# Layer 0's rotation of K: one product less, and its swapped half made by four SyncE copies; K cut a step sooner, Q a step later

## The reference

```python
Q = (query @ Wq.T).reshape(B, Tq, N_HEADS, D_K).transpose(0, 2, 1, 3)
K = (key @ Wk.T).reshape(B, Tk, N_HEADS, D_K).transpose(0, 2, 1, 3)
V = (value @ Wv.T)...
def apply_rope(x, cos, sin):
    x1 = x[..., 0::2]
    x2 = x[..., 1::2]
    r1 = x1 * c - x2 * s
    r2 = x1 * s + x2 * c
Q = apply_rope(Q, cos_q, sin_q)
K = apply_rope(K, cos_k, sin_k)
scores = jnp.einsum('bhqd,bhkd->bhqk', Q, K) / math.sqrt(D_K)
attn = jax.nn.softmax(scores, axis=-1)
out = jnp.einsum('bhqk,bhkd->bhqd', attn, V)
return out.transpose(0, 2, 1, 3).reshape(B, Tq, D_MODEL) @ Wo.T
```

## Time and profile before

| | |
|---|---|
| time, median of 3 runs | 532.25 us (531.01 to 532.5) |
| time of the profiled execution | 530.89 us |
| its span, first to last instruction | 529.1 us |
| mean granted TensorE clock | 0.947 |
| busy: PE, PE weight loads | 453.4 us (86%), 348.9 us (66%) |
| busy: DVE, ACT, POOL | 377.4 (71%), 348.2 (66%), 336.8 us (64%) |
| SyncE's DMA queue | 95666 packets, 45.06 MB, 34.6% of 16 engines |

### The profile page before, as it was taken

How to read it: one execution, slowest core, us unless ns; L and a number is a source line. 1 busy time by engine, 2 the same in 40 slices (tenths; PEclk the granted TensorE clock), 3 DMA queues, 4 the chain that set the end, 5 groups by cost and what they waited for, 6 DMA issues and landing times.

```text
span 529.1 us, 19004 instructions
## 1 busy us (share of the span) xinstructions
PE 453.4 (86%) x6103; PEld 348.9 (66%) x6103; DVE 377.4 (71%) x1113; ACT 348.2 (66%) x892; POOL 336.8 (64%) x710
## 2 busy tenths in 40 slices
PE   2688899999987888998799999999988615999992
PEld 2456677777765777997456666566655405999991
DVE  6787887888888557864567888898987562555551
ACT  4356788888876455664267788788875714666660
POOL 5787987788763346766444674888887670555552
PEclk9788999999999999999789999999998956999996
DMA  7556455555551720453222232243331133444430
GB/s 180 144 138 157 116 143 129 139 130 144 132 123 43 242 45 1 78 118 92 59 53 61 75 75 70 78 109 100 95 83 60 64 121 92 108 107 107 106 99 21
DMA packets 99108, 53.43 MB, mean 101 GB/s; under 512 B 25235, under 2 KB 96035, under 8 KB 99027
## 3 DMA queue, kind: packets, MB, share of 16 engines
q1 hardware_dynamic: 95666, 45.06, 34.6%
q0 software_dynamic: 2784, 6.82, 3.7%
q10 hardware_dynamic: 576, 0.53, 0.4%
HBM read 17.89 MB, written 8.81 MB: 50 GB/s over the span
## 4 chain that ended last, share of the span: by engine, by line
PE 62%; DVE 10%; DMA 9%; issue 6%; POOL 6%; SPq 3%; ACT 2%; ACTq 0%; DVEq 0%; POOLq 0%
PE bank L738 10%; PE bank L965 6%; PE score L686 6%; PE scoreT L955 4%; DMA stack<-negpT 4%; PE bank L873 4%; DVE negmax L1603 4%; PE scoreT L863 3%; DMA stack<-pieces 3%; PE score L651 3%; PE bank L787 3%; PE bank L600 3%; PE score L955 2%; PE scoreT L661 2%; PE scoreT L713 2%
## 5 line engine op out<-in xcount | busy, mean ns | idle before, releaser
L1603 DVE TENSOR_REDUCE negmax<-score 128x8 f32<-128x1024 f32 x128 | 156.3, 1221 | 46.2 <-PE score L686 45.2
L1077 ACT ACTIVATE P<-scoreT 128x1024 f32<-128x1024 f32 x128 | 131.2, 1025 | 48.2 <-PE scoreT L704 26.6
L738 PE MATMUL bank<-P,Vc 128*32 128x128 f32 x2048 | 71.7, 282 | 1.3 <-issue 0.8
L1517 POOL DMA_INDIRECT out<-by x39 | 37.4, 960 | 48.2 <-DVE by L1963 47.2
L738 PEld LDWEIGHTS bank<-P,Vc 128*32 128x32 f32 x2048 | 53.8, 112 | 15.5 <-issue 12.1
L686 PE MATMUL score<-stack 64*128 64x128 bf16 x896 | 45.8, 223 | 8.6 <-DMA stack<-pieces 4.3
L686 PEld LDWEIGHTS score<-stack 64*128 64x128 bf16 x896 | 26.1, 96 | 38.7 <-issue 22.1
L1358 POOL TENSOR_TENSOR negp<-negmax,blank 128x16 bf16<-128x16 f32 x64 | 14.1, 220 | 55.5 <-DVE negmax L1603 53.9
L965 PE MATMUL bank<-M,P 128*128 x312 | 41.4, 276 | 0.5 <-DVE by L1963 0.5
L1250 ACT ACTIVATE P<-scoreT,We 128x128 f32<-128x128 f32 x104 | 29.7, 369 | 15.3 <-PE scoreT L955 15.3
L965 PEld LDWEIGHTS bank<-M,P 128*128 128x128 f32 x312 | 38.0, 192 | 0.7 <-issue 0.7
(11 more groups left out here) (220 smaller groups left out, 1210.2 us busy)
## 6 DMA issues: line engine op xcount, KB each, us to landing
stack<-pieces SPq DMA_DIRECT2D x96, 128.0 KB, 2.6
stack<-pieces SPq DMA_DIRECT2D x96, 64.0 KB
XB<-expert_rows SPq DMA_DIRECT2D x39, 66.0 KB, 1.9
XA<-expert_rows SPq DMA_DIRECT2D x39, 64.0 KB, 1.9
XR<-in_x SPq DMA_DIRECT2D x4, 512.0 KB, 4.7
ctxT<-in_ctxT SPq DMA_DIRECT2D x16, 128.0 KB, 2.3
stack<-blank SPq DMA_DIRECT2D x32, 64.0 KB, 2.2
stack<-negpT SPq DMA_DIRECT2D x64, 32.0 KB, 1.9
```

Of the source, the lines that this page charges most:

```text
L738: mm = nc.tensor.matmul(PVOUT[VCOL * i:VCOL * (i + 1), half * 128:(half + 1) * 128], Vc[:, k % BODY, at:at + VCOL], P32[:, 2 * p_slot(L, k ...
L1077: nc.scalar.activation(P32[:, at:at + 2, :], SCORET[:], ACT.Exp, scale=SCALE).then_inc(sem("exp_done"), 1)
L1517: nc.gpsimd.indirect_dma_start(out=out, out_offset=bass.IndirectOffsetOnAxis(ap=at_, axis=0), in_=by[r][:, 0:D], in_offset=None).then_inc( ...
L1603: nc.vector.tensor_reduce(negmax[:, k % 2, :, half * HQ:(half + 1) * HQ], SCORE[:].rearrange("p r (h k) -> p r h k", h=HQ), AX.X, ALU.max, ...
```

## The change

K's product with the swapped weights is gone. The channels of a head are laid out even ones first (`EVEN_FIRST`), so that a channel's neighbour lies 32 partitions away. VectorE multiplies K's one product by a table with the opposite sign (`sinN`, a new input and load) and by cosT, the sine first. SyncE then copies the four blocks of 32 partitions of the sine product into a new tile `turned`, each block into its neighbour's place (`turn_keys`), and GpSimd adds `rotA` and `turned`. Q keeps two products.

K's product is written two steps sooner in the program and its cut one; Q's cut is one step later; the stack slots that need only K's later pieces go first. The context load is two steps sooner and waits for the value product of batch t + 4. The transposes of the normalised x move from the middle of the odd step to the end of the even one; ScalarE's work on them and on V moves accordingly. VectorE's cut of the first K is gone. SyncE's loop runs one round less, with the rest written out.

```diff
@@ SyncE
                         if L == 0:
-                            sp.wait_ge(sem("k_pieces"), middle)
+                            sp.wait_ge(sem("k_pieces"), low)
+                        sp.wait_ge(sem("q_pieces"), middle)
                         for s in LAST_SLOTS:
...
+                def turn_keys(k):
+
+                    p = pair(k)
+                    if is_pair(p):
+                        sp.wait_ge(sem("k_rotated"), known(2 * p + 1))
+                        sp.wait_ge(sem("k_full"), known(p + 0))
+                        for to in range(0, 128, TURN):
+                            at = to ^ TURN
+                            sp.dma_start(turned[to:to + TURN, :], rot[at:at + TURN, 3, :]).then_inc(sem("k_turned"), 16)
...
                     max_rows(t + 1, j + 1)
+                    if L == 0 and isinstance(t, int) and t == -AHEAD:
+                        load_ctx(j + 8)
                     if j % 2 == 1:
                         if L == 0:
-                            load_ctx(j + 7)
+                            turn_keys(j + 7)
+                            load_ctx(j + 9)
                             load_adj(j - 1)
@@ TensorE
-                def project_k(k, half):
+                def project_k(k):
...
+                        pe.wait_ge(sem(f"ctx_loaded{L}{b}"), 16 * turns(k))
+                        pe.wait_ge(sem("q_rotated"), 2 * p)
+                        nc.tensor.matmul(QK[:, 0:PAIR], W0[:, 2, :], ctxT[b][:], start=True, stop=True).then_inc(sem("k_projected"), 1)
...
-                    if L == 0 and j % 2 == 1:
-                        xn_transposes(j + 7, t)
...
-                        project_k(j + 6, 0)
-                        project_k(j + 6, 1)
+                        project_k(j + 8)
+                        xn_transposes(j + 8, t)
@@ ScalarE
-                        high(j + 4, 1)
+                        high(j + 4, 0)
+                        normalise(j + 8, (0, 1) if isinstance(t, int) and t == -AHEAD else (1,))
                     elif L == 0:
-                        high(j + 5, 0)
+                        high(j + 5, 1)
+                        evac_xnT(j + 7, t)
@@ GpSimd
                         pool.wait_ge(sem(f"{nm}_rotated"), 2 * p + 2)
+                        if which == 1:
+                            pool.wait_ge(sem("k_turned"), 64 * p + 64)
...
-                        cut(j + 4, 1)
+                        cut(j + 4, 0)
                     else:
-                        cut(j + 5, 0)
+                        cut(j + 5, 1)
...
-                            whole(j + 6, 0)
+                            whole(j + 6, 1)
                         else:
-                            whole(j + 5, 1)
+                            whole(j + 5, 0)
@@ VectorE
-                    for tab, dst, off in ((cosT, rotA, 0), (sinT, rotB, PAIR)):
+                    if which == 1:
+                        dve.wait_ge(sem("k_turned"), 64 * p)
+                    turns_ = ((sinT, rotB, PAIR), (cosT, rotA, 0)) if which == 0 else ((sinN, rotB, 0), (cosT, rotA, 0))
+                    for tab, dst, off in turns_:
...
-                        rotate(j + 5, 1)
+                        rotate(j + 7, 1)
```

More of the change, by code:

```diff
@@ L42 @@
 TILE = 64
+TURN = 32
 VW = DK + 1
@@ L114, in build @@
         sinT = sb("sinT", [128, 128])
-        W0 = sb("W0", [128, 5, 128])
+        sinN = sb("sinN", [128, 128])
+        W0 = sb("W0", [128, 4, 128])
         WV = sb("WV", [128, D + KV])
@@ L432, in stack_first @@
                             sp.wait_ge(sem("k_high"), high)
-                        sp.wait_ge(sem("q_pieces"), middle)
+                            sp.wait_ge(sem("k_pieces"), middle)
                         for s in FIRST_SLOTS:
@@ L493, in _ @@
             sp.wait_ge(sem("zeros_set"), 1)
-            body_loop(sp, step, START, {-2: partial(load_x_chunk, 2), 1: partial(load_x_chunk, 3), 3: load_late})
+            body_loop(sp, step, START, {-2: partial(load_x_chunk, 2), 1: partial(load_x_chunk, 3), 3: load_late}, nb=NB - 1)
             for dst, src in expert_loads:
@@ L569, in attention @@
                 NORM = (2, 4)[L]
-                WQ, WO = (W0[:, 0, :], W0[:, 4, :]) if L == 0 else (W1Q[:], W1X[:])
+                WQ, WO = (W0[:, 0, :], W0[:, 3, :]) if L == 0 else (W1Q[:], W1X[:])
                 def xn_transposes(k, t):
@@ L592, in project_q @@
                             pe.wait_ge(sem("xnT_ready"), p + P0 + 1)
[L594 to L597, removed]
+                            if L == 0:
+                                pe.wait_ge(sem("k_rotated"), 2 * p + 2)
                             else:
@@ L1170, in step @@
                     evac_outs(t - 1)
-                    if L == 0 and j % 2 == 1:
-                        evac_xnT(j + 7, t)
-                    exps(t, 1, j)
                     if L == 0:
@@ L1324, in attention @@
                 T0, P0 = L * B, L * PAIRS
-                def by_vector(p, which):
-                    return L == 0 and which == 1 and isinstance(p, int) and p == 0
                 def whole(k, which):
                     p = pair(k)
-                    if is_pair(p) and not by_vector(p, which):
+                    if is_pair(p):
                         nm = "qk"[which]
                         pool.wait_ge(sem(f"{nm}_rotated"), 2 * p + 2)
+                        if which == 1:
+                            pool.wait_ge(sem("k_turned"), 64 * p + 64)
                         pool.wait_ge(sem(f"{nm}_pieces"), count(3 * (p + P0)))
-                        nc.gpsimd.tensor_tensor(full[which][:], rotA[which], rotB[which], ALU.add).then_inc(sem(f"{nm}_full"), 1)
+                        nc.gpsimd.tensor_tensor(full[which][:], rotA[which], (rotB[0], turned[:])[which], ALU.add).then_inc(sem(f"{nm}_full"), 1)
                 def cut(k, which):
                     p = pair(k)
-                    if is_pair(p) and not by_vector(p, which):
+                    if is_pair(p):
                         nm = "qk"[which]
@@ L2105, in _ @@
             experts()
+EVEN_FIRST = list(range(0, DK, 2)) + list(range(1, DK, 2))
 def rope_tables():
@@ L2159 @@
         "x": g["x"], "ctxT": g["ctx_1024"].reshape(B * S, D).T, "mask": g["mask_BxSxS2_ik1"],
-        "W0": np.stack([wq[order].T, wq[swap].T, wk[order].T, wk[swap].T, g["L0_xattn_Wo"].T[packed]]),
+        "W0": np.stack([wq[order].T, wq[swap].T, wk[order].T, g["L0_xattn_Wo"].T[packed]]),
         "WV": np.concatenate([g["L0_xattn_Wv"][packed].T, g["L1_xattn_Wk"][order1].T, g["L1_xattn_Wv"].T], axis=1),
-        "cosT": cosT, "sinT": sinT, "eye": np.eye(128, dtype=np.float32),
+        "cosT": cosT, "sinT": sinT, "sinN": -sinT, "eye": np.eye(128, dtype=np.float32),
         "eyeb": np.eye(128).astype(ml_dtypes.bfloat16),
```

58 lines of the change are left out of this document (16 added, 42 removed).

## The result

The kernel after takes 572.47 us (median of 4 runs, 571.07 to 574.65) beside 531.99 us (4 runs, 531.01 to 532.5) for the kernel before: a ratio of 1.0773, 95% interval 1.0746 to 1.0801. The forecast was 567 us, with a range of 553 to 581.

A forecast was written before the change was run, and what follows sets the result against it. TensorE was taken to bound layer 0's steady stretch, with SyncE's issue queue only some 0.3 us behind. Start 13.8, steady stretch 19.8 and last exchange 1.4 made 35 us on a 532.25 us median: 567 us, range 553 to 581.

The forecast's parts named there:

- leg O to E: SyncE's queue from an odd step's maxima row to the next even one's: claimed 6.4 us (5.8 to 6.9) after.
- leg E to O: From an even step's maxima row to the odd step's: a latency loop, claimed to stay 4.3 us.
- Step 1: K's second product gone: about 0.45 us of TensorE per pair, claimed to give nothing in layer 0's steady stretch.
- Step 2: Four exchange copies per pair on SyncE's queue: 0.54 us each with gap, 2.2 us together (1.6 to 2.7).
- Step 3: TensorE's clock lowered after the new 2 us gap ahead of P·V: 0.3 us per pair.
- Rival C: TensorE at the lower clock in nearly every pair, with issues of 0.6 us: 578 us (573 to 587), chance 20%.
- Step 4: Start: early exchanges ahead of the loads; first stack copies +13.5 us, maxima row of 61.80 +13.8 us.
- Step 5: Moved cuts, transposes, earlier K and the context load's new wait: little price, over 1 us of cover for the exchange's landing.
- The last exchange: Issued behind the steady stretch's last maxima row, in a leg without a context load: about +1.4 us.
- A: SyncE's exchange issues near-free, under 0.08 us each: 532 us (528 to 536), no change or faster, chance 4%.
- B: Only the start costs as forecast, issues at the cheap end: 557 us (552 to 561), chance 23%.
- D: The start's delay is hidden or won back, the steady stretch's isn't: 553 us, chance 8%.

The follow-up runs named there:

- e5: Kernel before plus one dummy copy of 128 partitions (1 KB each) per pair on SyncE's queue: 532.53 us, ratio 1.0040.
- e11: Kernel before with K's second product simply left out, VectorE multiplying the one product by both tables: 538.70 us, ratio 1.0029.
- e1: Kernel after with x's second quarter, the small loads and two context loads issued ahead of the first exchange: 564.25 us, ratio 1.0607.
- e3: Kernel after with its moved steps alone: K's second product back and no exchange: 532.08 us, ratio 1.0024.
- e7: Kernel before plus four dummy copies per pair on SyncE's queue, each 32 partitions of 4 bytes: 564.98 us, ratio 1.0509.
- e8: Kernel after without exchange copies: VectorE writes the sine product in four 32-partition instructions straight into the neighbours' blocks: 541.18 us, ratio 1.0187.
- e4: Kernel before plus four dummy copies per pair on SyncE's queue, each 32 partitions of 1 KB: 560.25 us, ratio 1.0544.
- e2: Kernel after with the exchange as one plain copy of 128 partitions, blocks not changing places: 542.51 us, ratio 1.0236.
- e9: Kernel after with the exchange's four copies issued by ScalarE at its odd step's end instead of SyncE: 544.97 us, ratio 1.0262.

## Why the prediction was right, and where its sizes were off

**What bounds.** Right, with one omission. SyncE's queue was the near second bound in the leg O to E, and the slack that I read there was 0.3 us: in undisturbed pairs e5's one copy lengthened the leg from 4.36 us (106.40 to 110.76) to 4.66 (109.06 to 113.72), 0.3 of the 0.6 that an issue takes, so the 0.3 were there. On the mean of nine legs it was 0.48, which leaves some 0.2. But I called TensorE *the* bound of the steady stretch; e11 shows that in the leg E to O the latency loop bounds it nearly as much.

**Step 1, the product.** "Gives nothing here" fits the changed kernel, whose TensorE waits 17.1 us for maxima rows, and e11 says more than I claimed: on the kernel before it gives nothing measurable either.

**Step 2, four issues.** The mechanism held, the term was too small. I took 0.54 us with its gap; measured were, by line of the changed kernel:

```profile
L468 SPq DMA_DIRECT2D turned<-rot x64: 507/591/1444, 11.3 to 183.8; - x64
```

With gaps 2.49 us for four, so 0.62 each, near the upper end (2.7) of my range. The nearest row was not the maxima row (0.54) but layer 1's key rows (0.601 in the earlier trace rows), whose source also is 32 partitions. The leg O to E became 6.77, not 6.4: 9 x 0.37 = 3.3 us, the largest of the errors. It stayed inside 5.8 to 6.9. The pair took 11.48 us, over the 11.3 from which the prediction told the reader to look at the clock and at landings; the next step does.

**Step 3, the clock.** I took 0.3 us a pair, as a mean over pairs of which only some fall. The leg E to O is 4.71 against the 4.6 of the sum, +1.0 us over nine. The granted clock fell in three pairs of nine. Against the kernel before (4.32) the leg is 0.39 us longer. So clock and the one late landing told of below hold 3.5 us at most in this leg, and the rest of the 24.1, 20.6 us, lies in the leg with the issues. TensorE's timeline of four P·V products behind gaps, and two stretches by engine, the first behind the gap of 3.77 us, the other without a gap ahead of it (PEclk is the third number from the end):

```profile
88.60 0.40 PE L720 MATMUL scoreT<-stack 64*128 64x128 bf16 x8 [3.77 <-DMA stack<-negpT]
88.93 1.87 PE L745 MATMUL bank<-P,Vc 128*32 128x128 f32 x32
...
112.37 0.40 PE L720 MATMUL scoreT<-stack 64*128 64x128 bf16 x8 [2.03 <-DMA stack<-negpT]
112.69 1.75 PE L745 MATMUL bank<-P,Vc 128*32 128x128 f32 x32
...
124.84 0.40 PE L720 MATMUL scoreT<-stack 64*128 64x128 bf16 x8 [2.41 <-DMA stack<-negpT]
125.17 1.08 PE L745 MATMUL bank<-P,Vc 128*32 128x128 f32 x32
...
136.16 1.35 PE L745 MATMUL bank<-P,Vc 128*32 128x128 f32 x32
```

```profile
88.50:91.00 2.50, 2.40 (x42) 1.93 (x43) 0.00 (x0) 1.02 (x1) 0.00 (x0) 0.61 0.48 128
...
105.00:107.50 2.50, 2.50 (x66) 1.97 (x68) 2.19 (x5) 2.29 (x7) 2.34 (x6) 1.00 0.22 58
```

Rival C's mechanism is real, but in a third of the pairs. In one of the nine something else came on top: the maxima row issued at 84.70 let TensorE start only at 88.60, 3.9 us later, where it is 2.1 otherwise (133.76 to 135.83), and that leg took 7.0 us. Why that landing was so late I can't say.

**Step 4, the start.** 13.5 us were forecast at the first stack copies and 14.1 measured; exchange 0 was forecast at 11.3 and went out at 11.29. But at step 5 it was 16.2, not 13.8: my walk through the queue won back all four further exchanges, and 2.1 us of them were lost. "0 to 2 us on top" stood there, and I took the lower end. The rows of step 5 above show the split: 8.6 us are the order of the loads (e1 undoes 1.7% by it alone).

**Step 5, the small edits.** Right: e3 gives 0.24% (0.01 to 0.48) for all that is moved, and the exchange was waited for once, 1.2 us. One wait isn't in the prediction: the context load, now behind the four copies, held up K's product six times, 3.7 us in total. After it TensorE still waited for the maxima row, so no run shows a price for it.

**The last exchange.** 1.4 us forecast, and the leg behind the row of step 23 took 5.78 us (181.25 to 187.03), 1.3 more than before (4.44). Behind it 0.7 were won back, so that 0.6 are left at the end.

**The sum.** Forecast 13.8 + 19.8 + 1.4 = 35.0; measured 16.2 + 24.1 + 0.6 = 40.9. The steady stretch's 4.3 us too little are 3.3 of issues and 1.0 of the leg E to O.

**The rivals.** A (near-free issues) fell: no issue of a quarter of an exchange was under 0.5 us. The Trainium skill, page "DMA: Bandwidth & Descriptors", section on the anatomy of one DMA, gives about 50 ns for a dispatch on GpSimd's path; the trace doesn't agree for SyncE's queue: the exchange's issues show 507 ns at least and 591 in the median, e7's with 4 bytes a partition 592, and the measurement decides. B had the wrong end of the range, D fell with the first stack at 29.23. C had the sizes of the issues right and took the clock too heavily.

No kernel beat the one before. The best that keeps the exchange away from TensorE and does all of it is e8, 1.9% slower.

## What to carry to other kernels

Before moving work to a DMA, count issues and not bytes, and find the leg of the issuing queue into which they go: the price is some 0.6 us for each, less what that leg has to spare. The issuing queue can be the bound while its transfers are nowhere in the way. If one copy of all partitions can't do it, four copies are no substitute for it. An engine that is 99% busy isn't thereby the only bound: look for the latency loop beside it before pricing an instruction less as time gained.

## What the runs showed of the hardware

- An issue between two places in SBUF held SyncE for 592 ns at 4 bytes a partition and at 1 KB a partition alike (e7, e4), and one of 128 partitions for 602 ns (e5); but e2's copy of 128 partitions, between other tiles, took 522 ns in the median. ScalarE's issues cost no less, 613 ns in the median and 0.65 us each with gaps (e9). What ScalarE was already executing ran on beside them; the next instruction started only 0.1 us behind the last issue (111.76 and 111.86).
- VectorE takes 420 ns for 256 columns on 32 partitions and 421 ns on 128, and can write its result to another block of 32 partitions than the one that it reads (e8).
- After gaps of 3.77, 2.03 and 1.90 us TensorE's products ran slow, after gaps of 2.41 and 1.87 us (the latter ahead of 158.26) at full speed: the length of the last gap alone doesn't tell whether the clock falls.
